# Projections of all batches in the setup of layer 2, three-term, kept in scratch memory

## The reference

```python
# _L1_xattn_ref(layernorm(x), ctx, mask, ...), 16 heads of 32
q = w8a8_linear(x, wq, bq)      # rows and weights rounded to 8-bit integers, whole-number product, scaled
k = cond @ wk.T + bk
v = cond @ wv.T + bv
scores = einsum('bhnd,bhld->bhnl', q, k) / sqrt(32) + mask
o = einsum('bhnl,bhld->bhnd', softmax(scores), v)
x = x + tanh(g) * w8a8_linear(o, wo, bo)
# _L1_ffn_ref(layernorm(x), W1, W2): W1 512 -> 2048, W2 back
h = silu(bitlinear(x, W1))      # rows to 8 bits, weights to -1, 0, 1 times their mean magnitude
x = x + tanh(g) * bitlinear(h, W2)
```

## Time and profile before

| | us |
|---|---|
| median of 3 runs | 1078.93 |
| lowest, highest | 1077.7, 1079.21 |
| the profiled execution | 1081.88 |
| its span (first to last instruction) | 1080.1 |
| PE busy in the span | 938.5 (87%) |
| DVE busy | 743.1 (69%) |
| ACT busy | 555.1 (51%) |

### The profile page before, as it was taken

The page is one execution under the profiler, slowest core; times in us unless marked ns, Lnnn a source line. Parts: engine busy times, 40 slices in busy tenths (PEclk is TensorE's granted clock), DMA queues, the critical chain, the costliest instruction groups (busy, mean ns, idle before and its releaser), DMA issues.

```text
span 1080.1 us, 16123 instructions
## 1 busy us (share of the span) xinstructions
PE 938.5 (87%) x5776; PEld 621.2 (58%) x5784; DVE 743.1 (69%) x1925; ACT 555.1 (51%) x1104; POOL 72.6 (7%) x53
## 2 busy tenths in 40 slices
PE   3999879999999977569989889998989998899567
PEld 2777767767767654356644456644566544566333
DVE  5887863361626058479978688786699796799564
ACT  3444412221212137358854679845689647689243
POOL 4444100000000000000010000010000010000100
PEclk9999989999999998879999999999999999999869
DMA  6331400010203066861017820019420149300001
GB/s 214 117 117 39 156 1 1 32 48 1 78 1 117 1 214 237 192 156 41 2 39 157 195 78 2 4 53 208 128 79 2 40 86 197 108 2 2 1 0 40
DMA packets 45888, 85.99 MB, mean 80 GB/s; under 512 B 7409, under 2 KB 7409, under 8 KB 44785
## 3 DMA queue, kind: packets, MB, share of 16 engines
q1 hardware_dynamic: 42448, 80.24, 26.9%
q0 software_dynamic: 576, 4.19, 1.1%
q10 hardware_dynamic: 2784, 0.54, 0.3%
HBM read 43.01 MB, written 8.39 MB: 48 GB/s over the span
## 4 chain that ended last, share of the span: by engine, by line
PE 33%; DVE 10%; SPq 6%; issue 6%; DMA 5%; ACT 4%; POOL 0%; POOLq 0%; DVEq 0%; ACTq 0%
PE psum L1309 7%; PE psum L1326 6%; PE psum L1284 5%; PE psum L1382 5%; PE psum L1352 5%; SPq L962 5%; DMA k<-k_lo 4%; ACT probs L1110 2%; PE psum L1251 1%; PE psum L1368 1%; DVE amax L1531 1%; SPq L973 1%; DVE probsT L1619 1%; DVE xn L1699 1%; PE psum L1335 1%
## 5 line engine op out<-in xcount | busy, mean ns | idle before, releaser
L1110 ACT ACTIVATE probs<-psum,neg_max 128x512 f32<-128x512 f32 x256 | 174.8, 692 | 32.1 <-DVE neg_max L1593 32.0
L1593 DVE CUSTOM_DVE_ANT_0 psum<-psum,m_in 128x512 f32<-128x512 f32 x256 | 174.0, 702 | 18.5 <-issue 18.5
L1309 PE MATMUL psum<-ident,probs 128*128 128x128 f32 x1024 | 154.0, 274 | 0.0
L1309 PEld LDWEIGHTS psum<-ident,probs 128*128 128x128 f32 x1024 | 127.4, 141 | 21.0 <-issue 3.3
L1284 PE MATMUL psum<-k,q 128*128 128x512 f32 x256 | 125.9, 497 | 13.4 <-ACT probs L1110 8.3
L505 PE MATMUL psum<-w_sb,hT 128*128 128x512 f32 x256 | 115.1, 593 | 0.0
L389 ACT ACTIVATE hT<-psum,b_col 128x256 f32<-128x256 f32 x64 | 26.8, 470 | 136.2 <-PE psum L425 136.2
L1619 DVE COPY probsT<-psum 128x512 f32<-128x512 f32 x128 | 87.7, 685 | 2.6 <-PE psum L1309 2.3
L423 PE MATMUL psum<-xselT_hi,w_hi 128*128 128x256 f32 x256 | 82.8, 323 | 4.2 <-ACT onehotT L383 4.2
L1101 ACT COPY probsT<-psum 128x512 f32<-128x512 f32 x128 | 75.1, 587 | 19.8 <-PE psum L1309 19.8
L945 POOL TENSOR_TENSOR xres<-xres,xn 128x512 f32<-128x512 f32 x16 | 19.9, 1274 | 876.4 <-DVE xn L1699 876.4
(11 more groups left out here) (207 smaller groups left out, 1685.5 us busy)
## 6 DMA issues: line engine op xcount, KB each, us to landing
c_in<-in_ctx_dram SPq DMA_DIRECT2D x8, 1024.0 KB, 5.4
bw_in<-in_L_ffn_W_dram SPq DMA_DIRECT2D x8, 1024.0 KB, 11.2
k<-k_hi SPq DMA_DIRECT2D x32, 256.0 KB, 6.8
k<-k_lo SPq DMA_DIRECT2D x32, 256.0 KB, 8.5
q<-q_hi SPq DMA_DIRECT2D x64, 128.0 KB, 2.7
q<-q_lo SPq DMA_DIRECT2D x64, 128.0 KB, 2.4
xres<-in_x_dram SPq DMA_DIRECT2D x4, 1024.0 KB, 5.3
w_raw<-in_L_ffn_w_dram POOLq DMA_DIRECT2D x4, 1024.0 KB, 5.1
```

The costliest lines, as they stand in the source:

```text
L1110: act.activation(probs[:, u % 4, :], psum[u % SCORE_BANKS][:, :], ACT.Exp, scale=-1.0, bias=neg_max[:, u:u + 1], accum_out=prob_sum[:, nt, ...
L1309: mm = pe.transpose(turn_bank(u)[:, l * P:(l + 1) * P], probs[:, u % 4, l * P:(l + 1) * P], ident[:, :])
L1593: dve.tensor_tensor_reduce(bank[:, :], bank[:, :], m_in[:, nt, :], -1.0, LOWEST, ALU.add, ALU.min, neg_max[:, u:u + 1]).then_inc(masked_re ...
```

## The change

1. The projections of all four batches are made in the setup, by a new step `project(b)` on PE, ACT and DVE. `attend` and the tail hold none of it; every batch now has the tail that only the last one had.
2. Key and value weights and the context are split into high and low parts (F32R), and each key or value matmul becomes three (`three`): high by high, high by low, low by high.
3. Keys, queries and values go to scratch tensors in DRAM (`k_dram`, `q_dram`, `v_dram`), by transfers that POOL issues. SP loads `k4` and `q4` from there by groups of 4 heads, 4 transfers of 256 KB for each group and tensor, during the attention of the batch before, and `vv` too.
4. There is one `bw_in` in place of two. ACT rounds all four chunks (`round_chunks`), DVE clips them (`clip_chunk`), and PE transposes them straight from `bw_in`: `bw1` is summed in `project(0)` and turned in `project(1)`, `bw2` in `project(2)` and `project(3)`.
5. The matmuls with the values come in four bursts of 4, every second unit.

```diff
@@ PE
+                def three(dst, left, right, start, stop):
+                    (l_hi, l_lo), (r_hi, r_lo) = left, right
+                    pe.matmul(dst, l_hi, r_hi, start=start, stop=False)
+                    pe.matmul(dst, l_hi, r_lo, start=False, stop=False)
+                    return pe.matmul(dst, l_lo, r_hi, start=False, stop=stop)
...
+                def keys(b, tiles):
+                    for o in tiles:
+                        if o >= 2:
+                            pe.wait_ge(k_lo_ready, b * CT_ + o - 1)
...
+                def values(b, t):
+                    if t >= 2:
+                        pe.wait_ge(v_ready, b * T + t - 1)
+                    else:
+                        pe.wait_ge(q_scaled, b * CT_ + t + 1)
...
+                def project(b):
+                    if b:
+                        pe.wait_ge(q_scaled, b * CT_)
+                    keys(b, range(3))
+                    query_rows(b)
+                    keys(b, range(3, CT_))
+                    queries(b)
+                    if b % 2:
+                        turn_bw(b // 2)
+                    for t in range(T):
+                        values(b, t)
+                        if b + 1 < B:
+                            context(b + 1, (t,))
+                    if b % 2 == 0:
+                        pe.wait_ge(sxrow_ready, b + 1)
+                        bw_sums(b // 2)
@@ ACT
+                def project(b):
+                    normed_queries(b)
+                    key_highs(b, range(2))
+                    if b == 0:
+                        magnitude(0, 0)
+                    rounded_queries(b)
+                    key_highs(b, range(2, 3))
+                    query_scales(b)
+                    turned_rows(b, (2, 3))
+                    key_highs(b, range(3, CT_))
+                    if b % 2 == 0:
+                        for k in range(1 if b == 0 else 0, 4):
+                            magnitude(b // 2, k)
+                    query_highs(b)
+                    if b % 2:
+                        turned_bw(b // 2)
+                    if b + 1 < B:
+                        turned_context(b + 1, range(CT_))
+                    if b % 2 == 0:
+                        round_chunks(b // 2)
+
+                def attend(b):
+                    act.wait_ge(q_saved, 32 * B)
@@ DVE
+                def project(link, b):
+                    query_scales(link, b)
+                    for c in range(CT_):
+                        key_low(b, c)
+                        if b % 2 and c < 2:
+                            clip_chunk(b // 2, c)
+                    scaled_queries(b)
+                    if b % 2:
+                        clip_chunk(b // 2, 2)
+                        clip_chunk(b // 2, 3)
+                    query_lows(b)
+                    if b % 2:
+                        turned_bw(b // 2)
+                    for t in range(T):
+                        biased_value(b, t)
+                        if b + 1 < B:
+                            context_low(b + 1, t)
+                            if t == 2:
+                                query_stats(link, b + 1)
+                    if b % 2 == 0:
+                        bw_unit(link, b // 2)
+                    if b + 1 < B:
+                        query_root(link, b + 1)
@@ POOL
+                for b in range(B):
+                    save_keys(b)
+                    save_values(b)
+                    save_queries(b)
@@ SP
+                load_context(0)
                 for k in range(4):
-                    sp.dma_start(bw_in[0][:, k, :].rearrange("p (t c) -> p t c", t=FT // 4),
+                    sp.dma_start(bw_in[:, k, :].rearrange("p (t c) -> p t c", t=FT // 4),
...
+                    if k == 0:
+                        load_rows(0)
```

More of the change, by code:

```diff
@@ L802, in layer1 @@
         probsT = at("probsT", [P, 2, HPG, T, 2 * P], F32, arena)
[L803 to L811, removed]
@@ L995, in _ @@
[L995 to L1008 removed]
+                sp.wait_ge(ctxT_psum, CT_)
@@ new lines, in _ @@
+                load_context(1)
+                sp.wait_ge(sh.x2_stored, 16 * B)
+                sp.wait_ge(qxT_psum, 2)
+                load_rows(1)
+                sp.wait_ge(ctxT_psum, 2 * CT_)
+                load_context(2)
+                sp.wait_ge(qxT_psum, 4)
+                load_rows(2)
+                for k in range(4):
+                    sp.wait_ge(bwT_psum, 2 * k + 2)
+                    sp.dma_start(bw_in[:, k, :], bw2[P * k:P * (k + 1), :]).then_inc(bw_loaded[1][k], 16)
@@ new lines, in context @@
+                def context(b, tiles):
+                    pe.wait_ge(c_loaded, b * 16 + 16)
+                    for c in tiles:
+                        if c == 3:
+                            pe.wait_ge(ctxT_lo_ready, b * CT_ + 1)
+                        for t in range(T):
+                            mm = pe.transpose(psum[CONTEXT_BANKS[c]][:, t * P:(t + 1) * P], c_in[:, t, c * P:(c + 1) * P],
+                                              ident[:, :])
+                        mm.then_inc(ctxT_psum, 1)
@@ new lines, in query_rows, with queries @@
+                def query_rows(b):
+                    pe.wait_ge(sx_ready, b + 1)
+                    for t in range(T):
+                        mm = pe.transpose(psum[7][:, t * P:(t + 1) * P], scale_q[:, t:t + 1].to_broadcast([P, P]), ident[:, :])
+                    mm.then_inc(sxrow_psum, 1)
+                    if b:
+                        pe.wait_ge(v_ready, b * T)
+                    pe.wait_ge(xnq_rounded, b * T + T)
+                    turn_rows(xn, (2, 3))
+                def queries(b):
+                    pe.wait_ge(qxT_ready, b * 2 + 2)
+                    for o in range(CT_):
+                        if o >= 2:
+                            pe.wait_ge(k_lo_ready, b * CT_ + o + 1)
+                        for c in range(CT_):
+                            mm = pe.matmul(psum[(2, 3, 0, 1)[o]][:, :], wqT[:, c, o * P:(o + 1) * P], qxT[:, c, :],
+                                           start=(c == 0), stop=(c == CT_ - 1))
+                        mm.then_inc(q_psum, 1)
@@ L1316, in attend @@
                                     pe.wait_ge(pT_ready[k], b * (UNITS // 2) + (hg + 1) * UH // 2)
-                                if more and hg == HG - 1:
-                                    context(b + 1, c_in)
+                                if hg == 0:
+                                    pe.wait_ge(vv_loaded, 16 * (b + 1))
                                 if hg >= 2:
@@ L1456, in _ @@
+                pe.wait_ge(w_lo_ready, 2 * CT_)
+                for t in range(CT_):
+                    mm = pe.transpose(psum[7][:, t * P:(t + 1) * P], sh.w_scale[:, 1, t:t + 1].to_broadcast([P, P]), ident[:, :])
+                mm.then_inc(linear_psum, 1)
+                pe.wait_ge(swo_ready, 1)
+                for b in range(B):
+                    project(b)
+                pe.wait_ge(v_ready, B * T)
                 first_scores(0)
-                for b in range(B - 1):
-                    batch(b, True)
@@ L1459, in _ @@
-                batch(B - 1, False)
+                for b in range(B):
+                    batch(b)
             @block.vector
```

715 lines of the change are left out of this document (313 added, 402 removed).

## The result

The changed kernel takes 1188.2 us (median of 4 runs, 1186.62 to 1189.77), the kernel before 1078.32 us on the same chip: 1.102 times as long (95% interval 1.0996 to 1.105). Slower, as forecast, and 6 us above the forecast of 1182. The profiled execution took 1189.77 us, its span is 1187.7 us, 107.6 more than before.

The account below looks back on a forecast made before the run. Waits between engines were taken to bound the layer 2 setup, PE the attention. Profiled 1081.88 us, +141 for later first exponentials, -38 for tails, gave 1184.9, as median 1182 us; range 1150 to 1212.

Parts of the forecast that it names:

- The tails, -38: Tails of three batches: each loses the next batch's projections, 12.7 us, so 38 us less in all.
- The beginning: Start of the layer 2 setup: x lands one megabyte later, so keys start at 416.3 us, against 400.30 before.
- The walk: Setup, the four `project(b)`: following which engine waits for whom, keys at 416.3 lead to the last value tile at 585.
- two additions: Setup: 5 us for handovers and 10 us for the slow clock, added to the 585 reached by following the waits.
- The slow clock and the handovers, +10 and +5: Setup: PE slower after stalls, 1.5 to 2 us each, 10 in all; results later over some 25 handovers, 5 us.
- The saves, +14: End of setup: ACT's first exponentials wait for POOL's saves of batch 3, 14 us, ends 5.1 and 20.
- the engines are shared: End of setup: POOL's three 1 MB saves share transfer engines with SP's loads, so 14 us between 5.1 and 20.
- The loads ... I cost them at nothing: Attention: loads now running beside it touch no engine's instructions, 0 us; a late group would wait before unit 16, 32 or 48.
- the sum (1184.9): Whole kernel, against the profiled execution: 1081.88 + 141 - 38 = 1184.9 us; the median of runs 3 us below, 1182.
- The bursts, 0: Attention: finer bursts win at best 20 us or cost 13; taken as 0.
- PE as the bound of the setup (1123): Rival, setup: other engines keep ahead and each `project` costs PE's 28.5 us, giving 1123 us; 7 in 100.
- Starving saves: Rival, setup: DVE's clips and copies hold back POOL's saves, so queries come late, giving 1205 to 1225 us; 6 in 100.

Follow-up runs that it names:

- experiment 3: Changed kernel with SP loading x of batch 0 before the loads of `k4` and `q4`: 1181.87 us, ratio 1.0979 to the kernel before.
- experiment 1: Changed kernel with three of ACT's four roundings of `bw_in` in odd batches moved behind the fourth high key: 1184.4 us, ratio 1.1006 to the kernel before.
- experiment 11: Changed kernel with the fp8 copies of `bw1` and `bw2` ahead of the high and low queries in odd batches: 1183.62 us, ratio 1.0998.
- experiment 6: Changed kernel with DVE making the low parts of weights and context 0 before it waits for x of batch 0: 1182.55 us, ratio 1.097.
- Experiment 10: Changed kernel with SP's loads of `k4` and `q4` beyond the first group held until all POOL's saves have landed: 1199.64 us, ratio 1.113.
- experiment 9: Changed kernel with POOL saving the last queries ahead of the last values and SP loading x of batch 0 first: 1163.55 us, ratio 1.0802.
- experiment 4: Changed kernel with the value matmuls in two bursts of 8 per 8 units, as before the change: 1189.41 us, ratio 1.1057.
- experiment 12: The kernel before with only the value matmuls changed, to four bursts of 4: 1078.01 us, ratio 1.0027.
- experiment 7: Changed kernel with one matmul (high by high) in place of three for each key and value step: 1168.19 us, ratio 1.0836.
- experiment 5: Changed kernel with SP's last 8 loads of `q4` and the load of x held until all POOL's saves have landed: 1189.83 us, ratio 1.1042.

## Why the prediction was right

- **The tails, -38.** Mechanism right, size nearly so: 13.6 and 13.3 us in batches 1 and 2, for 12.7. In batch 0 it was there too, but a wait covered it: with x loaded first (experiment 3) it came out, at 12.9.
- **The beginning.** Keys were to start at 416.3 and started at 413.27. 2.3 us of that gap are no part of the change: this execution began layer 2 earlier (PE's weight transposes at 388.58, before at 390.91). Counted from there, x landed 12.1 us later in place of 9.35, so 2.7 us later as forecast (402.9 for 400.26), and keys started 24.7 us later where 25.4 were forecast.
- **The walk.** Key tile 2 of batches 1, 2 and 3 came by the walk at 464.4, 509.3 and 551.5, and in the trace at 462.02, 511.03 and 557.78, each released by DVE's low keys as written down; the turning waited too, 5.56 us twice. PE stood still for 3 us or more five times from there on, for the six or seven of the prediction. From the start of keys to the first scores the walk with its two additions gives 183.7 us and the trace 181.0. Experiments 1, 11 and 6 moved the waits it names.
- **The slow clock and the handovers, +10 and +5.** Together 12.3 us and not 15, since the walk without them gave 168.7. In the traces that show 184.1 to 184.6 us for this stretch it would be 15.4 to 15.9. Behind a wait the key tiles 2 of batches 1, 2 and 3 take 4.35, 5.28 and 4.26 in place of 2.73 us, and value tile 2 of batch 2 takes 4.44: 7.4 us of the 12.3, 1.5 to 2.6 each for the 1.5 to 2 of the prediction. Their beginning ran at a granted clock of 0.50. How the other 4.9 divide is not separated. The start and this made the first scores come at 594.31 and not at 600.
- **The saves, +14, were too little**: 19.2 us. The step that failed is "the engines are shared", priced by a middle value: 6 MB of loads had been issued ahead of the saves, and more than half was still to come (2.7 MB can have landed at 210 GB/s). What was left of them, 3.6 MB, and the saves, 3.1 MB, are 6.7 MB; from 595 to 614 the DMA engines moved 339 GB/s, 6.4 MB. So the last save landed about when the backlog did, which as an estimate is the price: bytes outstanding over the rate. Experiment 10, with next to nothing ahead, gives 10.4 us, and the same saves of batch 0 took 11.4. The page "DMA: Bandwidth & Descriptors" of the Trainium skill (Anatomy of one DMA) gave 9.2 us as an estimate for the three on end; that is near the 10.4 and the 11.4, and doesn't hold behind a queue of loads, where the single transfers took 11.7, 14.5 and 17.6 us.
- These two errors, -6 and +5, cancel: the first exponentials were forecast at 614 and came at 613.71. That is luck, the more so as 2.3 of the -6 come from layer 1. A right total was here not proof of its terms.
- **"The loads ... I cost them at nothing"** failed in one place. During the attention it holds. But `x_in` of batch 0 stood behind 32 loads in SP's queue, and DVE waited 6.3 us for it; experiments 3 and 9 show it. Batch 0 so saved 5.7 us for 12.7, 7.0 too little, and the other batches 2.1 more than forecast: that is the 4.9 us by which the profiled execution (1189.77) lies above the sum (1184.9).
- **The bursts, 0:** right; experiments 4 and 12 bound them at a few us.
- **The rivals.** PE as the bound of the setup (1123) is out by the 10.8 us waits and by experiment 7, although three terms do cost 20 us. Starving saves, after the page "SBUF — State Buffer" (SBUF: two separate sides) of the Trainium skill, are out in this kernel: the saves were slowest while DVE stood idle (2.04 us of work in 19) and the DMA engines were full. That page's rule isn't contradicted, only not met.

## What to carry to other kernels

Work taken out of a tail whose own waits hid more than half of it (32 plain matmuls of 0.87 us are 28 us of PE, and 13 came back) gives back little, and the same work in a setup pays its full chain: walk the written order engine by engine, and price each wait by what stands ahead of its releaser. Where a transfer's landing is on the path, count the bytes issued before it on any queue, not only its own. And when a wait is to be removed, ask at once what is late next: removing the saves' wait alone gave 0, removing x's alone some 5, both 24 us.

## What the runs showed of the hardware

- **Full DMA engines move different amounts.** With only loads of 256 KB into `k4` and `q4`, each to 32 partitions, they showed a share of 0.96 and 210 GB/s (581 to 594), with saves among them 1.05 and 339 GB/s (595 to 614), and 416 GB/s in the best 5 us of experiment 5. A busy share says that the engines are taken, not what they deliver. The saves come from all 128 partitions. Why the loads alone are slower stays open; their form was not varied.
- **Less work for PE can lower its granted clock.** In experiment 7 the granted clock from the start of keys to the first scores was 0.76, where it was 0.88 in the changed kernel, and the key tile of 4 matmuls behind the wait of 13.34 us ran wholly at the lower level (0.50, 1.2 GHz): 2.08 us. The 4 products were over before the clock rose; with 12 behind a wait of 10.81 us the last 5 ran at full clock (4.35 us for the tile). The waits took more than the clock. As an estimate, the matmuls left out are 58 us at full clock (two thirds of 8 tiles of 2.73 us in each of four batches); PE's busy time fell by 50, so the clock took some 8, and the stretch by 21.9, so waits took the other 28.
- Four bursts of 4 cost some 0.3 us more of PE in 8 units than two of 8, and the loop's time moved by 0.03 (experiment 12) to 0.1 us (experiment 4): PE's idle time took it up. In 480 to 540 PE is busy 57.21 us in experiment 12, where it was 55.62.
